# A three-layer state-space scan: 112 groups written out instead of looped, and two loads moved or cut

## The reference

```python
for i in range(3):                      # the scan stage, three layers
    delta = softplus(W_dt * (x . w_dt) + b_dt)
    dA  = exp(delta[..., None] * -exp(A_log[i]))        # 64 channels x 64 states
    dBx = (delta * x)[..., None] * B(x)[:, :, None, :]
    h[t] = dA[t] * h[t-1] + dBx[t]                      # associative_scan over t
    x = einsum(h, C(x)) + D * x
    if i < 2: x = mean of neighbouring pairs of steps
h = x + s5_layer(layernorm(x))          # "mixing": a complex diagonal scan over t
h = h + expert_ffn(layernorm(h))        # each token goes through one of 32 experts
```

## Time and profile before

| | |
|---|---|
| median of 3 runs | 6189.39 us |
| lowest, highest | 6179.43, 6201.01 us |
| the profiled execution, its own time | 6180.16 us |
| its span | 6178.2 us |
| mean granted TensorE clock | 0.977 |
| instructions in the profile | 115644 |

### The profile page before, as it was taken

The page is one execution under the profiler, slowest core; times in us unless marked ns, Lnnn a source line. Parts: engine busy times, 40 slices in busy tenths (PEclk is TensorE's granted clock), DMA queues, the critical chain, the costliest instruction groups (busy, mean ns, idle before and its releaser), DMA issues.

```text
span 6178.2 us, 115644 instructions
## 1 busy us (share of the span) xinstructions
PE 4744.0 (77%) x36042; PEld 1959.5 (32%) x36042; DVE 5952.3 (96%) x4016; ACT 5011.7 (81%) x10247; POOL 5890.6 (95%) x996
## 2 busy tenths in 40 slices
PE   6777777777777777777777777777777777777789
PEld 2333333333333333333333333333333333333234
DVE  8999999999999999999999999999999999999965
ACT  7888888888888888888888888887888888888844
POOL 8999999999999999999999999999999999999933
PEclk8999999999999999999999999999999999999999
DMA  7888888888878888878788888888888888878710
GB/s 252 270 261 269 264 268 262 265 263 266 263 263 265 268 269 261 269 262 270 264 269 269 269 269 269 261 269 265 262 267 263 268 267 272 270 265 271 253 41 14
DMA packets 562114, 1567.59 MB, mean 254 GB/s; under 512 B 172113, under 2 KB 320530, under 8 KB 561298
## 3 DMA queue, kind: packets, MB, share of 16 engines
q1 hardware_dynamic: 561426, 1559.30, 77.6%
HBM read 1468.37 MB, written 90.59 MB: 252 GB/s over the span
## 4 chain that ended last, share of the span: by engine, by line
DVE 53%; issue 26%; POOL 11%; PE 6%; DVEq 1%; DMA 1%; SPq 1%; ACT 1%; ACTq 0%; POOLq 0%
DVE hT L930 53%; POOL u L1137 11%; PE decay L553 2%; DVEq L929 1%; PE decay L611 1%; PE prep_bank L631 1%; DVE dx L941 1%; PE z_bank L418 1%; PE decay L400 1%; DMA u<-dx_rows 1%; ACT decay L716 0%; PE decay L617 0%; PE prep_bank L451 0%; SPq L290 0%; DVEq L928 0%
## 5 line engine op out<-in xcount | busy, mean ns | idle before, releaser
L1137 POOL TENSOR_TENSOR u<-u,Bt 128x2976 f32<-128x2976 f32 x896 | 5783.5, 6504 | 87.3 <-DMA u<-dx_rows 86.8
L930 DVE TENSOR_TENSOR_SCAN hT<-decay,u 128x744 f32<-128x744 f32 x3584 | 5741.9, 1677 | 78.3 <-ACT decay L716 66.0
L716 ACT ACTIVATE decay<-decay,a_neg 128x371 f32<-128x371 f32 (+2 forms) x7168 | 3606.4, 546 | 628.5 <-PE decay L400 590.7
L400 PE MATMUL decay<-stk,spread 96*128 96x371 bf16 (+2 forms) x7168 | 1794.2, 333 | 1387.1 <-DVE hT L930 1177.5
L418 PE MATMUL z_bank<-hT,Cst 128*32 128x256 f32 x21472 | 1474.2, 392 | 1.4 <-issue 1.1
L400 PEld LDWEIGHTS decay<-stk,spread 96*128 96x128 bf16 x7168 | 419.7, 98 | 2885.2 <-DVE hT L930 2720.3
L725 ACT COPY z_sb<-z_bank 128x512 f32<-128x512 f32 x1342 | 791.8, 590 | 260.7 <-PE z_bank L418 260.3
L418 PEld LDWEIGHTS z_bank<-hT,Cst 128*32 128x32 f32 x21472 | 569.3, 110 | 680.3 <-issue 450.5
L428 PE MATMUL z_bank<-stk,spread 96*128 96x372 bf16 x1677 | 361.8, 325 | 0.0
L506 PE MATMUL prep_bank<-tmap,yT 64*128 64x32 f32 (+3 forms) x1344 | 213.9, 280 | 0.0
L506 PEld LDWEIGHTS prep_bank<-tmap,yT 64*128 64x128 f32 x1344 | 175.9, 188 | 108.7 <-issue 108.7
(11 more groups left out here) (140 smaller groups left out, 2537.5 us busy)
## 6 DMA issues: line engine op xcount, KB each, us to landing
u<-dx_rows SPq DMA_DIRECT2D x3584, 372.0 KB, 4.3
delta_parts<-parts SPq DMA_DIRECT2D x112, 279.0 KB, 6.6
stk<-delta_parts SPq DMA_DIRECT2D x112, 279.0 KB, 5.4
y_rows<-z_sb SPq DMA_DIRECT2D x1792, 12.0 KB
yT<-y_rows SPq DMA_DIRECT2D x112, 192.0 KB, 4.5
dx_rows<-dx SPq DMA_DIRECT2D x112, 186.0 KB, 2.6
xT<-in_x SPq DMA_DIRECT2D x64, 186.0 KB, 5.0
xP<-in_x SPq DMA_DIRECT2D x64, 186.0 KB, 4.4
```

The lines of the kernel that those rows point to most:

```text
L400: nc.tensor.matmul(slot[:, e, :, 1:], spread[0:PARTS * QR, TILES_G * q + er // TILES_G, :], src[:, er % TILES_G, :, 1:], start=True, stop= ...
L716: last = nc.scalar.activation(bank, bank, ACT.Exp, scale=a_neg[:, l, c:c + 1])
L930: nc.vector.tensor_tensor_scan(hT[q % 2][:, i * PAIR:(i + 1) * PAIR], pair_slot(turn, p), u[c % RING][:, part * PAIR:(part + 1) * PAIR], 0 ...
L1137: tt(here, here, Bt[buf][:, :].unsqueeze(1).broadcast_to([P, 2 * HALVES * CHUNK, W0]), ALU.mult).then_inc(s_u, 1)
```

## The change

Three edits. (1) `layer_bodies` no longer has a loop: each engine's program holds all 112 groups one behind the other, with constants where the loop took register values. (2) The load of h for the mixing stage, which was one transfer for chunks 0 to 13 and one for 14 and 15, becomes three: chunks 0 and 1, chunks 2 to 13, chunks 14 and 15, each with its semaphore; TensorE waits for them before chunk 0, chunk 2 and chunk 14. (3) x of group 1 is loaded at the end of the first loads, ahead of the store of group 0's `dx`, instead of in the body of group 0; the very first load of x gets a semaphore of its own.

```diff
+        m_h3 = [sem(f"m_h{i}_loaded") for i in range(3)]
...
+        def x_is_loaded(n):
+
+            return (s_x, 16 * n) if n else (s_x0, 16)
...
                 n = groups[l]
 
-                first = 2 + (n - 4) % ROUND_OF_GROUPS
-                for g in range(first):
-                    body(g % 2, turn(l, g), *group(l, g))
-                with eng.Fori(0, (n - 2 - first) // ROUND_OF_GROUPS) as k:
-                    for g in range(ROUND_OF_GROUPS):
-                        body(g % 2, turn(l, first + g), *group(l, ROUND_OF_GROUPS * k + (first + g)))
-                for g in range(n - 2, n):
+                for g in range(n):
                     body(g % 2, turn(l, g), *group(l, g))
...
-                sp.dma_start(xT[buf][:, :], source(at)).then_inc(s_x, 16)
+                sp.dma_start(xT[buf][:, :], source(at)).then_inc(s_x if n else s_x0, 16)
...
-                    if c == 4 and after:
+                    if c == 4 and after and after != (0, 1):
                         load_x(after, 1 - half)
...
+            load_x((0, 1), 1)
             store_dx(first, 0)
             layer_bodies(sp, body)
...
-            first = chunks - 2
+            first, last = 2, chunks - 2
             sp.wait_ge(s_diag, 16 * TB * G(LAST))
             sp.wait_ge(s_store, 16 * G(BEFORE_LAST))
-            sp.dma_start(h3[:, 0:first * W0], hs[-1][:, 0:first * W0]).then_inc(m_h3, 16)
+            for at, end in ((0, first), (first, last)):
+                sp.dma_start(h3[:, at * W0:end * W0], hs[-1][:, at * W0:end * W0]).then_inc(m_h3[at > 0], 16)
...
-            sp.dma_start(h3[:, first * W0:chunks * W0], hs[-1][:, first * W0:]).then_inc(m_h3, 16)
+            sp.dma_start(h3[:, last * W0:chunks * W0], hs[-1][:, last * W0:]).then_inc(m_h3[2], 16)
...
-                    pe.wait_ge(s_x, 16 * (n + 1))
+                    pe.wait_ge(*x_is_loaded(n))
...
-                    if isinstance(c, int) and c in (0, chunks - 2):
-                        pe.wait_ge(m_h3, 16 if c == 0 else 32)
+                    if isinstance(c, int) and c in (0, 2, chunks - 2):
+                        pe.wait_ge(m_h3[(0, 2, chunks - 2).index(c)], 16)
...
-                dve.wait_ge(s_x, 16 * (n + 1))
+                dve.wait_ge(*x_is_loaded(n))
```

More of the change, by code:

```diff
@@ L21 @@
 EPT = D // TILES_G
-ROUND_OF_GROUPS = 6
 SLOTS = 3
@@ L123, in tower @@
         s_aexp, s_aneg = sem("a_exp"), sem("a_neg_ready")
-        s_x, s_xP = sem("x_loaded"), sem("x_reloaded")
+        s_x0, s_x, s_xP = sem("first_x_loaded"), sem("x_loaded"), sem("x_reloaded")
         s_item, s_read = sem("item_written"), sem("item_read")
@@ L171, in tower @@
         s5c, col = z_flat[1][:, 700:703], z_flat[1][:, 704:728]
-        m_load, m_h3, m_small, m_expand = sem("m_weights_loaded"), sem("m_h_loaded"), sem("m_small_loaded"), sem("m_expand_cast")
+        m_h3 = [sem(f"m_h{i}_loaded") for i in range(3)]
+        m_load, m_small, m_expand = sem("m_weights_loaded"), sem("m_small_loaded"), sem("m_expand_cast")
         m_tab, m_acol, m_abig, m_chain, m_tables = (sem("m_tables_step"), sem("m_cols_exp"), sem("m_sins"),
```

## The result

The changed kernel takes 6112.59 us (median of 4 runs, 6110.93 to 6118.68) against 6191.4 us for the kernel before (4 runs, 6179.43 to 6201.01): a ratio of 0.9879, 95% interval 0.9861 to 0.9896. The forecast was 6108 in a range of 6098 to 6132. The profiled execution took 6110.93 us (span 6109.1), 69 us less than the profiled one before; 74.6 were forecast.

A forecast was written before the change was run, and what follows sets the result against it. VectorE was taken as the bound, with GpSimd nearly as full, losing time at 13 loop jumps. Gains of 66.8 + 3.1 + 4.7 = 74.6 us from 6180.16 gave 6105.6, plus part of a 9.2 us offset: 6108 us, range 6098 to 6132.

The forecast's parts named there:

- The bound and the price of a jump: Scan stage: VectorE, at 51.585 us a group, bounds it; each of 13 loop jumps costs 5.2 us.
- the 0.3 of group 0: Group 0 to group 1: 0.3 us of the 67.1 us lost, counted as no jump's.
- The 66.8 us for the jumps: Scan stage: writing out all groups removes 13 jumps and gains 66.8 us; register arithmetic counts nothing.
- Nothing else becomes late: Scan stage without jumps: the next bound is VectorE's own 51.585 us a group.
- it keeps up by a hair: GpSimd in the scan stage: eight tiles take 51.5 us a group when free, against VectorE's 51.585.
- x of group 1: Head of the stage: early x brings VectorE's second scan to about 35.6; gain 3.1 us, bounds 0 and 3.4.
- rival 3: Stage faster, but head or tail gives nothing: 6113.4 us, or 6122.6 with the full offset; chance 0.10.
- The load in front of the others: Head: the added early transfer on SyncE costs nothing, or 0.6 us without cover.
- h in three parts: Start of the mixing stage: TensorE's first product moves from 5886.77 to about 5882.1; gain 4.7 us, bounds 0 and 4.7.
- the 2.4 us that I added for the spread of the runs: Whole kernel: about a quarter of the median's 9.2 us over the profiled run, kept since jumps may cause part of the spread.
- written-out code that runs dry for lack of instructions: Scan stage: late fetches at 5.0 us each; 20 stalls give 6206 us (chance 0.03), 5 to 10 give 6130 to 6156 (0.05).
- The branch's own price as the whole cost: Scan stage: a branch costs about 108 ns, the pauses stay, only head and tail gain: 6172.4 us; chance 0.03.

The follow-up runs named there:

- experiment 6: The changed kernel with the load of x for group 1 put back in the body of group 0: 6114.88 us.
- experiment 1: The changed kernel with the loop of six groups put back on all engines, early x and three parts of h kept: 6177.62 us.
- the two kernels with the extra matmuls: The changed kernel with three useless TensorE matmuls at pair 23 of each group: 6112.61 us; with GpSimd's first tile also in two halves: 6107.84 us.
- experiment 2: The changed kernel with the loop put back on all engines at twelve groups a round, so 5 jumps: 6136.63 us.
- experiment 5: The changed kernel, all groups written out, with a tiny loop of two rounds on each engine at the 13 old jump places: 6111.58 us.
- its repetition: The changed kernel run once more, unaltered, beside the last two kernels: 6114.12 us.

## Why the prediction was right

*The bound and the price of a jump* are confirmed: the time follows the number of far jumps (0, 5, 13) at about 5 us each, near ones cost nothing, and register code costs nothing. The price was read as 67.1 / 13 = 5.2; the 13 groups with a jump are 64.9 us longer in all, 5.0 each. The other 2.2 are the 0.3 of group 0 and a stall of the granted clock (1.9 us, group 18) that I counted as the jumps'. In one of the 13, group 81 (7.1 us over), a half clock of 13.7 us begins ahead of the jump, so a second such stall may stand in it.

*The 66.8 us for the jumps* were over by 7.3; 59.55 were gained. The step that was mis-sized is "Nothing else becomes late". The changed kernel has three stalls of the granted clock, 5.7 us; they are why VectorE still waits 4.9 us for decays, where under 3 were forecast. And "it keeps up by a hair" was the weak sentence: it took 38.66 us for six tiles, 51.5 for eight, as free pace, and GpSimd's pace in the stage is 51.62. GpSimd has no lead to live on; that costs 1.9 us. Together they are 7.6, and the 0.3 of group 0 that was kept out of the forecast went as well. It takes two of the edits to lose the lead. In the kernel before it is 3.7 us in group 1, from VectorE's wait for the late x, and the bursts renew it; it never falls below 1.6. With the jumps gone but the late x kept (experiment 6) it starts at 3.6 and no pace is lost; with the early x but the jumps kept (experiment 1) it starts at 0.1 and is 4.6 by group 8. With both edits made it is 0.09 until the changed kernel's first stall. So the 1.9 us belong to the two edits together.

*x of group 1*: 3.1 forecast, 3.4 measured inside group 0. Here the same 1.9 us can be read as the price: the edit pulls VectorE level with GpSimd, and that much of the gain is returned in the groups behind it. Undone, it makes no difference to the time that can be measured, so for this edit rival 3 comes close. The load in front of the others was costed at nothing, and nothing shows that it cost anything.

*h in three parts*: 4.7 forecast and 4.7 measured between the two profiles; against one load in the written-out kernel 5.7. That part of rival 3 is out. The prediction took the matmuls of the first steps to run at the lower clock and gave two rows for it. Only the first shows it (two in 1.58 us); four in 1.49 us is the full clock. The clock there is worth the 2.2 us that the mixing stage gained, within the 3 that were allowed.

*The sum*: 3.4 - 0.7 (a later first landing) + 59.55 + 4.7 + 2.2 (the mixing stage's clock) = 69.1, the difference of the spans. Forecast 74.6. That the median came within 5 us of 6108 is in part luck: the 2.2 us of the mixing stage were in no term, and the 2.4 us that I added for the spread of the runs made up for part of the rest. The reason for adding them, that the spread belongs partly to the jumps, is not shown. Runs of the kernel before lie 21.6 us apart and those of the changed kernel 7.8, but with six-group loops ten runs lie 13.1 apart, and the two kernels with the extra matmuls, whose profiles have no clock stalls, 1.6 and 2.3. That points to the clock's stalls.

*The rivals*: written-out code that runs dry for lack of instructions did not appear. The new stalls are of another kind, and 5.7 us. The branch's own price as the whole cost is out by experiments 1, 2 and 5. "Slightly fewer" bytes of instructions was too cautious: 6.1 MB instead of 8.3.

Open is why TensorE's stop is longer when other engines jump too (2.8 us of kernel time for either side, 5.0 for both); how much of a far jump's price is the half clock behind it; and what makes the half clock last 13.7 us in some groups and 3.4 in others at the same pair.

## What to carry to other kernels

A loop with a long body (here six groups, some 310 us) paid a fixed price of 5 us at each jump back. What seems to count is how many instructions each engine jumps over: engines stopped with some 480 and more between two jumps, and did not with 317 (TensorE), 135 (GpSimd, twelve groups a round) or fewer; what lies between was not tried. Look for one burst per round in the idle time of the engine that bounds the kernel: fewer and longer rounds help in proportion, and short loops don't need to be written out. When two engines are equally full, a stall of one is the other's lead. Take the stalls away and the slower of the two sets the pace, so cost both at their pace in the stage, not at their free pace.

## What was not expected of the hardware

- The stops at a far jump lengthen each other: TensorE's is 4.39 us when it jumps alone and 6.08 us when all five engines do. The added time lies ahead of its fetch's own transfer (2.1 us against 3.7).
- GpSimd makes the same jump over six groups, 68 instructions of its own, and does not stop (0.24 to 0.29 us).
- The granted clock halved for 13.7 us behind pairs 21 to 23, in which TensorE has idle time, in three groups of the changed kernel and five of its repetition; three more matmuls per group there ended the stalls.
- The mixing stage's length, 289.2 to 294.3 us, goes with how long the granted clock is half in its first 50 us.
- GpSimd's tile takes 6.44 us in the first group and 6.45 (51.62 / 8) in the stage, enough to set the pace.
